# Cross-attention's output product on 13 flat tiles of 128 tokens, fed through memory

## The chip, the core and the metric

One core of a Trainium2 chip runs the whole program. The metric is the device time of one execution, in microseconds (us). TensorE is called PE below, VectorE DVE, ScalarE ACT, GpSimd POOL, and SyncE, which issues most of the DMAs, SP. A matrix product is TensorE's `lhsT.T @ rhs`: `lhsT` is loaded first (its width, up to 128 columns, is the height of the result), then `rhs` streams through, one column after the other.

## What is computed

A decoder layer on 16 batches of 100 tokens, 512 wide: self-attention, cross-attention to a context of 361 tokens per batch, and a mixture-of-experts feed-forward, each with a residual and a layer norm. The change is in the middle one, and in how its tokens are numbered for the last one:

```python
x = _layernorm(x + _L0_attn_ref(x, w_q, w_k, w_v, w_o))
# cross-attention, 16 query heads of 128 over 4 key/value heads
q = rmsnorm((x @ Wq + bq) split into 16 heads); k = rmsnorm(ctx @ Wk + bk); v = ctx @ Wv + bv
scores = einsum('bhsd,bhed->bhse', q, k) / sqrt(128)
out = einsum('bhse,bhed->bhsd', softmax(scores + mask), v)       # [16, 16, 100, 128]
x = _layernorm(x + out.reshape(16, 100, 2048) @ Wo)              # Wo: [2048, 512]
# feed-forward: logits = x @ router_w + router_b, the two best of 8 experts for each token,
# silu(x @ expert_w + expert_b), weighted sum, proj, residual, rms norm; then layernorm
```

## The kernel before, in words

Three phases follow each other: self-attention (to about 430 us of the trace), cross-attention (to about 1256 us), feed-forward. Each engine runs its own list of instructions in program order, and they meet at semaphores. Every float32 product of cross-attention is made of three matmuls (`product3`, line 67 on; the matmul is L75): each operand is split into a high and a low part in fp32r, and high times high, high times low and low times high are added in the PSUM bank.

Cross-attention is written as `body(j, par)` for batch j = 0 to 15, with a last, short `body(16, 0)`. A batch has four **steps** s = 0 to 3, one for each key/value head with its four query heads; step n = 4j + s counts them through. In step n PE does:

- for each of the four heads: `scores` into one of two banks, `transpose_probs` (L946) of one chunk of the probabilities of step n - 1, and a filler, `quarter(q)`;
- products for the keys of the next batch (`keys`, chunk 1 in the quarters of step 2, chunk 0 in step 1, chunk 2 at the end of step 2), their transposes (`transpose_keys`, L986, in steps 2 and 3), and the values of this batch (`values`, step 0);
- `values_product(n - 1)`, probabilities times values, into `o_bank`.

DVE and ACT take that bank apart into `b_oTh` and `b_oTl` (L1164 on ACT, L1299 on DVE, which adds to `o_lo`), laid out [128, 4, 400]: head width on the partitions, four heads of 100 tokens of one batch. `output(j, kv, heads)` multiplies them with `Wo`: for each batch 16 heads of three matmuls, `lhsT` 128x100, `rhs` 128x512, added up in `y_bank`. The 16 heads of a batch lie as fillers: 4 in the quarters of step 0 and 4 in those of step 1 (heads of the batch before), 1 in step 2, 7 in step 3.

The softmax of step n: `masked` on DVE (L1227, row maximum), `exponent` on ACT (L1113), `invert_sums` on DVE (L1233), `normalise` on POOL (L1402), and then PE may transpose in step n + 1. Between heads 2 and 3 DVE also does `queries(n + 1)` (L1238): it scales the queries of the next step, which SP's `load_q` (L872, L873) has loaded; ACT and POOL split them (L1119, L1391). In step 2 DVE then runs `key_squares(j + 1, 1)`, whose first instruction (L1190) empties the bank that `keys(j + 1, 2)` on PE waits for (`k_ev`).

In SP's list of before `load_q(n + 1)` waits only for the scores of step n - 1 (`s_done`). Each batch ends with `residual_norm` and `apply_norm` on DVE, the store of x2, and, two batches later, `transpose_x2` (L1006) and `logits` (L1013) on PE, all on 100 rows. The feed-forward ranks the logits, counts places for 16 batches of 100 tokens, and gathers rows of x2 by expert; the chosen places go through memory (`pick_d`) from [100, 16] to [128, 13].

Of the kernel before, what the change touches and what calls it, by code (L numbers as in the profile page):

```python
# [26 lines left out]
P = 128  # L27
# [28 lines left out]
ROUTE_WIDTHS = (S, P, NJ, E * E, NT, B)  # L56
ROUTE_COLS = sum(ROUTE_WIDTHS)
ROUTE_SPANS = [(sum(ROUTE_WIDTHS[:k]), sum(ROUTE_WIDTHS[:k + 1])) for k in range(len(ROUTE_WIDTHS))]

# [684 lines left out]
def cross_attention_phase(nc, sem, head, stage, ctxT, Wo, bv, mask, ident_s, router_w, router_b, route_c, expert_w, Ehl, x1_d, q_d, rs_d, x2_d):  # L744
# [6 lines left out]
    with ExitStack() as ctx:  # L751
# [13 lines left out]
        mask_s = sb("b_mask", [S, SE])  # L765
# [5 lines left out]
        carry = sb("b_carry", [S, XG + 1])  # L771
# [6 lines left out]
        with nc.sbuf_tensor("b_equal", [S, (B - 1) * E * E], F32) as equal_s:  # L778
            pass
        kTh = sb("b_kTh", [P, 2, XKV, SEP + 1], F32R)  # L780
        with nc.sbuf_tensor("b_above", [S, (B - 1) * E * E], F32) as above_s:
            pass
# [5 lines left out]
        oTh, oTl = sb("b_oTh", [P, XKV, XG * S], F32R), sb("b_oTl", [P, XKV, XG * S], F32R)  # L788
        x1_s, y_s = sb("b_x1", [S, D]), sb("b_y", [S, D])
        stat, mv, rstd = sb("b_stat", [S, 6]), sb("b_mv", [S, 2]), sb("b_rstd", [S, 1])  # L790
# [15 lines left out]
        y_done, ysum, stat_set, mv_set = sem("b_y_done"), sem("b_ysum"), sem("b_stat_set"), sem("b_mv_set")  # L806
# [8 lines left out]
        rb_s = stage[0:S, 0, 0, DC * E:(DC + 1) * E]  # L815
        x2T = stage[:, 0, 1, 0:DC * S]
# [25 lines left out]
        def routed(j):  # L842

            return not (isinstance(j, int) and j < 2)
# [16 lines left out]
        def _(sp):  # L861
# [20 lines left out]
            sp.dma_start(mask_s[:], mask).then_inc(consts, 16)  # L882

            def body(j, par):
                first, last, past = kinds(j)
                if not past:
                    load_q(4 * j + 1, 1, 16 * j)
                    if first:
                        load_weights(KV_PIECES)
                        load_weights(KV_PIECES + 1)  # L890
                    if not last:
                        load_ctx(j + 1, 0)
                        load_ctx(j + 1, 1)
                    load_q(4 * j + 2, 0, 16 * j + 4)
                    if first:
                        load_weights(KV_PIECES + 2)
                        load_weights(KV_PIECES + 3)
                    if not last:
                        load_ctx(j + 1, 2)
                    if last:  # L900
# [4 lines left out]
                    load_q(4 * j + 3, 1, 16 * j + 8)  # L905
                    if first:
                        load_weights(KV_PIECES + 4)
                        load_weights(KV_PIECES + 5)
                    wait(sp, ysum, j)
                    sp.dma_start(x1_s[:], x1_d[bass.ds(j, 1)].rearrange("a t d -> t (a d)")).then_inc(x1_in, 16)  # L910
                if not past and not last:
                    load_q(4 * j + 4, 0, 16 * j + 12)
                if not first:
                    sp.wait_ge(x2_rdy, j)
                    sp.dma_start(x2_d[bass.ds(j - 1, 1)].rearrange("a t d -> t (a d)"), y_s[:]).then_inc(x2_out, 16)
                if first:
                    load_weights(KV_PIECES + 6)
                    load_weights(KV_PIECES + 7)
                    sp.wait_ge(w_lo, len(pieces))
                    sp.dma_start(rw_s, router_w).then_inc(router_in, 16)  # L920
                    sp.dma_start(rb_s, router_b.partition_broadcast(S)).then_inc(router_in, 16)
                    sp.dma_start(cst, route_c).then_inc(router_in, 16)
            over_batches(sp, body)

        @block.tensor
        def _(pe):
# [63 lines left out]
            def output(j, kv, heads=range(XG)):  # L990

                if heads[0] == 0:
                    pe.wait_ge(o_lo, 4 * j + kv + 1)
                if kv == 0 and heads[0] == 0:
                    wait(pe, ysum, j)
                mm = product3(pe, y_bank[0:S, :], lambda h: oTh[:, kv, h * S:(h + 1) * S],
                              lambda h: oTl[:, kv, h * S:(h + 1) * S], lambda h: Woh[:, XG * kv + h, :],
                              lambda h: Wol[:, XG * kv + h, :], heads, first=kv == 0 and heads[0] == 0,
                              last=kv == XKV - 1 and heads[-1] == XG - 1)
                if kv == XKV - 1 and heads[-1] == XG - 1:  # L1000
                    mm.then_inc(y_done, 1)

            def transpose_x2(b):
                pe.wait_ge(x2_rdy, b + 1)
                for c in range(DC):
                    mm = pe.transpose(kv_bank[0][:, c * S:(c + 1) * S], y_s[:, c * P:(c + 1) * P], ident_s[0:S, 0:S])  # L1006
                mm.then_inc(rt_done, 1)

            def logits(b):
                pe.wait_ge(router_in, 48)  # L1010
                pe.wait_ge(rt_ev, b + 1)
                for c in range(DC):
                    mm = pe.matmul(kv_bank[0][0:S, DC * S:DC * S + E], lhsT=x2T[:, c * S:(c + 1) * S], rhs=rw_s[:, c, :],  # L1013
# [12 lines left out]
            def body(j, par):  # L1026
                first, last, past = kinds(j)
                for s in range(1 if past else 4):
                    n, before = 4 * j + s, not (first and s == 0)
                    now = not past  # L1030
                    def quarter(q):

                        if s < 2 and not first:
                            output(j - 1, s + 2, (q,))
                        if s == 2 and not last:
                            keys(j + 1, 1, (q,))
                        if s == 3:
                            output(j, (q + 1) // XG, ((q + 1) % XG,))

                    for h in range(3):  # L1040
# [9 lines left out]
                        if s == 0 and h == 0 and routed(j):  # L1050
                            transpose_x2(j - 2)
                        if s == 0 and h == 2 and routed(j):
                            logits(j - 2)
# [5 lines left out]
                    if s == 0 and now and not first:  # L1059
                        if routed(j):  # L1060
                            pe.wait_ge(lg_ev, j - 1)
                        values(j, 0)
                    if s == 1 and not last:
                        keys(j + 1, 0)
                    if s >= 2 and first:
                        pe.wait_ge(w_lo, KV_PIECES + 2 * (s - 1))
                    if s == 2:
                        output(j, 0, range(1))
# [3 lines left out]
                    if s == 3:  # L1072
                        output(j, 1, range(1, 2))
# [5 lines left out]
                    if s == 3:  # L1079
                        output(j, 1, range(2, XG))  # L1080
                if past:
                    output(j - 1, 3)
                    pe.wait_ge(lg_ev, B - 1)
                    transpose_x2(B - 1)
                    logits(B - 1)
                elif first:
                    pe.wait_ge(w_lo, len(pieces))
# [3 lines left out]
        def _(act):  # L1091
# [29 lines left out]
            def x2_transposed(b):  # L1121
                act.wait_ge(rt_done, b + 1)
                wait(act, lg_done, b)
                if isinstance(b, int) and b == 0:
# [1017 lines left out]
```

## Time and profile before

| | |
|---|---|
| time of 3 runs | 1463.97, 1468.15, 1470.35 us (median 1468.15) |
| the profiled execution: its own time, its span | 1479.52 us, 1477.7 us |
| busy share of the span: PE, DVE, ACT, POOL | 94%, 57%, 48%, 41% |
| mean granted TensorE clock | 0.976 of 2.4 GHz |
| DMA: moved, mean share of the 16 DMA engines | 126.56 MB, q1 (SP's queue) 24.3% |
| output product of cross-attention | 768 matmuls of 128x100 by 128x512 |

A busy PE isn't PE at its peak: the busy times of matmuls overlap, and what one costs is the distance from its start to the next one's. From 500 to 1200 us, 14 of the 16 batches, the profile repeats about every 50.1 us; the rows below are from one such batch.

### The profile page before, as it was taken

The numbers are of one execution on the slowest core, as the hardware profiler recorded it, in microseconds if no ns is written. First come the engines' busy times: TensorE is split into PE (matmuls) and PEld (weight loads), VectorE is DVE, ScalarE is ACT, GpSimd is POOL, SyncE is SP. The second block draws the span as 40 slices with busy tenths as digits, with TensorE's granted clock in tenths as the row PEclk, the third lists the DMA queues.
The fourth block names the chain that finished last, engine by engine and source line by source line (L and its number), as shares of the span: only waits on it lengthen the run. The fifth ranks groups of instructions, "written<-read, shape, count | busy, mean of one in ns | idle before, by whom it ended". The sixth has DMA issues, their size and how long they took to land. (4 is left out here: it accounts for less than half of the span.)

```text
span 1477.7 us, 24718 instructions
## 1 busy us (share of the span) xinstructions
PE 1390.1 (94%) x8497; PEld 1174.2 (79%) x8497; DVE 841.9 (57%) x3014; ACT 711.3 (48%) x1877; POOL 611.3 (41%) x940
## 2 busy tenths in 40 slices
PE   8999999999978999999999999999999997499976
PEld 7789888888857888888888888888888876377854
DVE  4553434344356667666755765576567655744357
ACT  5755555554434444444444444454445444343246
POOL 1632211121126455545544554545454535434154
PEclk9999999999988999999999999999999999699998
DMA  6212112122334221222121212211221130765362
GB/s 202 93 38 74 59 55 73 52 68 82 132 103 120 65 60 40 65 60 59 35 77 49 70 36 66 60 59 47 65 60 51 55 117 25 260 194 169 111 220 100
DMA packets 67475, 126.56 MB, mean 86 GB/s; under 512 B 11835, under 2 KB 42911, under 8 KB 66456
## 3 DMA queue, kind: packets, MB, share of 16 engines
q1 hardware_dynamic: 62776, 110.04, 24.3%
q0 software_dynamic: 4576, 14.95, 3.6%
q8 instruction: 69, 1.13, 0.3%
q14 instruction: 54, 0.44, 0.1%
HBM read 93.50 MB, written 31.45 MB: 85 GB/s over the span
## 5 line engine op out<-in xcount | busy, mean ns | idle before, releaser
L1113 ACT ACTIVATE b_probs<-b_probs,b_nmax 100x361 f32<-100x361 f32 x256 | 152.6, 596 | 68.7 <-DVE b_nmax L1227 67.4
L75 PE MATMUL bank<-b_kTh,b_q 128*100 128x362 f32 x512 | 172.7, 338 | 8.6 <-POOL b_q L1391 5.3
L1370 POOL TENSOR_TENSOR b_pcarry<-b_half 128x1 f32<-128x1 f32 x173 | 37.6, 217 | 343.7 <-DVE b_rinv L1233 322.0
L1227 DVE CUSTOM_DVE_ANT_0 b_probs<-bank,b_mask 100x361 f32<-100x361 f32 x256 | 135.4, 529 | 69.4 <-issue 61.4
L1108 ACT ACTIVATE b_pTh<-bank 121x400 fp32r<-121x400 f32 x192 | 95.8, 500 | 126.5 <-PE bank L946 125.6
L1402 POOL TENSOR_SCALAR b_probs<-b_probs,b_rinv 100x361 f32<-100x361 f32 x256 | 153.7, 613 | 0.0
L1220 DVE TENSOR_TENSOR b_pTl<-bank,b_pTh 121x400 fp32r<-121x400 f32 x192 | 109.7, 572 | 38.4 <-ACT b_pTh L1108 38.3
L946 PE MATMUL bank<-ident,b_probs 100*121 100x100 f32 x768 | 111.8, 268 | 7.6 <-POOL b_probs L1402 7.0
L946 PEld LDWEIGHTS bank<-ident,b_probs 100*121 100x121 f32 x768 | 106.0, 186 | 15.3 <-POOL b_probs L1402 12.5
L75 PE MATMUL bank<-b_Woh,b_oTh 128*100 128x512 f32 x256 | 110.8, 433 | 1.4 <-DVE b_oTl L1299 1.4
L440 ACT ACTIVATE a_probs<-a_probs,a_nmax 100x100 f32<-100x100 f32 x256 | 93.2, 366 | 36.7 <-DVE a_nmax L561 36.5
L1164 ACT ACTIVATE b_oTh<-bank,b_bv 128x400 fp32r<-128x400 f32 x64 | 38.1, 596 | 139.9 <-PE bank L75 139.9
L75 PEld LDWEIGHTS bank<-b_kTh,b_q 128*100 128x100 f32 x512 | 85.3, 167 | 22.9 <-POOL b_q L1391 6.8
L75 PE MATMUL bank<-b_Wol,b_oTh 128*100 128x512 f32 x256 | 100.8, 394 | 0.0
L75 PE MATMUL bank<-b_Woh,b_oTl 128*100 128x512 f32 x256 | 100.6, 393 | 0.0
L606 DVE TENSOR_SCALAR a_qb<-bank,a_bq,a_qkw 128x400 f32<-128x400 f32 x64 | 44.3, 693 | 94.6 <-PE bank L75 94.6
L75 PE MATMUL bank<-a_x1Th,a_Wqh 128*128 128x400 f32 x256 | 91.7, 358 | 0.2 <-ACT a_qsq L464 0.2
L75 PE MATMUL bank<-a_x1Tl,a_Wqh 128*128 128x400 f32 x256 | 88.3, 345 | 0.0
L75 PE MATMUL bank<-a_x1Th,a_Wql 128*128 128x400 f32 x256 | 88.3, 345 | 0.0
L706 POOL TENSOR_TENSOR a_probs<-a_probs,a_rinv 100x400 f32<-100x400 f32 x64 | 54.6, 855 | 73.0 <-DVE a_rinv L568 73.0
L75 PE MATMUL bank<-b_Wkh,b_ctxh 128*121 128x512 f32 x192 | 81.2, 423 | 3.5 <-DVE b_kn L1190 3.5
L75 PE MATMUL bank<-b_kTl,b_q 128*100 128x362 f32 x256 | 84.4, 330 | 0.0
(256 smaller groups left out, 3793.9 us busy)
## 6 DMA issues: line engine op xcount, KB each, us to landing
q_d<-a_qb SPq DMA_DIRECT2D x64, 200.0 KB, 2.4
b_q_raw<-q_d SPq DMA_DIRECT2D x64, 200.0 KB, 2.5
b_q_raw<-rs_d SPq DMA_DIRECT2D x64, 200.0 KB, 3.4
b_ctxr<-in_ctxT SPq DMA_DIRECT2D x48, 242.0 KB, 4.5
y_d<-c_y SPq DMA_DIRECT2D x32, 256.0 KB
c_Eraw<-in_expert_w SPq DMA_DIRECT2D x10, 512.0 KB, 7.4
a_stage<-in_Wq SPq DMA_DIRECT2D x4, 1024.0 KB
stage<-in_Wo SPq DMA_DIRECT2D x8, 512.0 KB, 4.5
```

The costliest lines, as they stand in the source:

```text
L75: mm = eng.matmul(out, lhsT=l(c), rhs=r(c), start=first and k == 0, stop=last and k == n - 1)
L440: e = act.activation(probs[:, r, c, :], probs[:, r, c, :], ACT.Exp, scale=-1.0, bias=nmax[:, h:h + 1], accum_out=psums[:, r, c:c + 1])
L606: dve.tensor_scalar(qb[:, u % 2, :, m % XG, :], q_bank(m)[:, 0:GT].rearrange("p (b t) -> p b t", b=GB), bq_s[:, m % XH:m % XH + 1], qkw_s[ ...
L706: pool.tensor_tensor(probs[:, r], probs[:, r], rinv[:, r].unsqueeze(2).to_broadcast([S, DC, S]), ALU.mult).then_inc(pn_rdy, 1)
L946: mm = pe.transpose(t_bank[c % 2][0:KT, h * S:(h + 1) * S], probs[:, s % 2, h, c * KT:(c + 1) * KT], ident_s[0:S, 0:S])
L1108: act.activation(pTh[:, c, :], t_bank[c % 2][0:KT, 0:XG * S], ACT.Copy).then_inc(pt_hi, 1)
L1113: act.activation(p, p, ACT.Exp, scale=-1.0, bias=nmax[:, s % 2, h:h + 1], accum_out=psums[:, s % 2, h:h + 1]).then_inc(e_rdy, 1)
L1164: act.activation(oTh[:, kv, :], o_bank[:, 0:XG * S], ACT.Identity, bias=bv_s[:, kv:kv + 1]).then_inc(o_hi, 1)
L1220: dve.tensor_tensor(pTl[:, c, :], t_bank[c % 2][0:KT, 0:XG * S], pTh[:, c, :].bitcast(F32), ALU.subtract).then_inc(pt_lo, 1)
L1227: dve.tensor_tensor_reduce(out=probs[:, s % 2, h, 0:SE], in0=s_bank[h % 2][0:S, 0:SE], in1=mask_s[:], scale=-1.0, scalar=BIG, op0=ALU.add, ...
L1370: pool.tensor_tensor(pcarry[:, k:k + 1], half_s[:, 0:1], half_s[:, 0:1], ALU.add)
L1402: pool.tensor_scalar(p, p, rinv[:, s % 2, h:h + 1], 1.0, ALU.mult, ALU.mult).then_inc(p_rdy, 1)
```

## The change

The output product no longer works batch by batch. The 1600 tokens are cut into 13 tiles that ignore batches: tile 0 has 64 rows (`SHORT`), the others 128. Since a tile takes rows of two or three batches, what `values_product` gives is stored in DRAM (`o_d`, `store_values`, after `o_lo`) and loaded back by tiles (`load_group` into `b_oD0`, `b_oD1`). A **group** is a tile and a key/value head: 4 heads, 12 matmuls with `lhsT` 128x128. `output_plan` gives each group a step, at most one in a step (two in step 63), none in a step 2 before step 36. Of the last tile only 28 columns come from memory; 100 are written in place. The residual, the norms, the transposes, the logits and the routing work on the 13 tiles with 128 partitions, and `pick_d` is gone.

```diff
+def output_plan():
+    order = [(t, kv) for t in range(NT) for kv in range(XKV)]
+    plan, g = {}, 0
+    while order:
+        plan[g] = []
+        room = 2 if g == 4 * B - 1 else 0 if g % 4 == 2 and g < 36 else 1
+        while order and room:
+            t, kv = order[0]
+            ready = 4 * last_batch(t) + kv + (2 if t == NT - 1 else 3)
+            if ready > g:
+                break
+            plan[g].append(order.pop(0))
+            room -= 1
+        g += 1
...
+            def load_group(t, kv):
+                k = slot(t, kv)
...
+                    wait(sp, y_grp, taken(t, kv))
+                if t < NT - 1:
+                    sp.wait_ge(o_out, 16 * (4 * last_batch(t) + kv + 1))
+                    src = o_d[kv][:, :, :, tile_start(t):tile_start(t) + tile_rows(t)]
+                    sp.dma_start(oD[k][:, :, :, 0:tile_rows(t)].bitcast(F32), src).then_inc(od_in[k], 16)
...
+            def store_values(n):
+                sp.wait_ge(o_lo, n + 1)
+                sp.dma_start(o_d[n % 4][:, :, :, n // 4 * S:(n // 4 + 1) * S], oT[:].bitcast(F32)).then_inc(o_out, 16)
...
+                for s in range(1 if past else 4):
+                    g = 4 * j + s
+                    if g + 1 < 4 * B:
+                        load_q(g + 1, (g + 1) % 2, 4 * g)
...
+                    for t, kv in PLAN.get(g + 1, ()):
+                        load_group(t, kv)
...
+                    if 1 <= g <= 4 * (B - 1):
+                        store_values(g - 1)
...
-                        if s < 2 and not first:
-                            output(j - 1, s + 2, (q,))
                         if s == 2 and not last:
                             keys(j + 1, 1, (q,))
-                        if s == 3:
-                            output(j, (q + 1) // XG, ((q + 1) % XG,))
+                        for t, kv in groups:
+                            if len(groups) > 1:
+                                if q % 2 == 0:
+                                    output(t, kv, (q, q + 1))
+                            elif s < 3 or q < 2:
+                                output(t, kv, (q,))
...
                     if s == 2:
-                        output(j, 0, range(1))
                         values_product(n - 1, s - 1, j)
...
-                    if s == 3:
-                        output(j, 1, range(1, 2))
                     if before and s != 2:
                         values_product(n - 1, (s + 3) % 4, j)
...
-                    if s == 3:
-                        output(j, 1, range(2, XG))
+                    if s == 3 and len(groups) == 1:
+                        for t, kv in groups:
+                            output(t, kv, range(2, XG))
...
-                    if s == 1 and not first:
-                        residual_norm(j - 1)
...
+                    if n in DONE[:-1]:
+                        residual_norm(DONE.index(n))
```

By the plan the groups lie: one in every step 0 from step 4 on but for 48, one in every step 1 from step 5 on but for 13 and 49, one in every step 3 (two in 63), and one in the steps 2 numbered 38, 42, 46, 54, 58 and 62; two more in steps 64 and 65. `DONE`, the steps in which a tile's last group lies, is 7, 12, 19, 24, 29, 35, 39, 43, 47, 54, 58, 62, 65.

PE, the end of a step 3, from the last matmul of the scores over `transpose_keys(2)` (reads `b_kn`) to the product with the values. Before:

```order
L75 MATMUL bank<-b_kTh,b_q 100x362
L986 MATMUL bank<-ident,b_kn 128x121 x4
L75 MATMUL bank<-b_Woh,b_oTh 100x512
L75 MATMUL bank<-b_Wol,b_oTh 100x512
L75 MATMUL bank<-b_Woh,b_oTl 100x512
L75 MATMUL bank<-b_Woh,b_oTh 100x512
L75 MATMUL bank<-b_Wol,b_oTh 100x512
L75 MATMUL bank<-b_Woh,b_oTl 100x512
L75 MATMUL bank<-b_pTh,b_Vh 128x400
```

The same place after:

```order
L122 MATMUL bank<-b_kTh,b_q 100x362
L1075 MATMUL bank<-ident,b_kn 128x121 x4
L122 MATMUL bank<-b_pTh,b_Vh 128x400
L122 MATMUL bank<-b_pTl,b_Vh 128x400
L122 MATMUL bank<-b_pTh,b_Vl 128x400
```

Two heads (six matmuls) between the key transposes and the product with the values are gone; a third is gone between scores 2 and 3.

SP, one batch of a middle part, from a step 1 to the next step 0. Before:

```order
L872 DMA b_q_raw<-q_d 128x400
L873 DMA b_q_raw<-rs_d 128x400
L868 DMA b_ctxr<-in_ctxT 128x484
L872 DMA b_q_raw<-q_d 128x400
L873 DMA b_q_raw<-rs_d 128x400
L910 DMA b_x<-x_d 100x512
```

After:

```order
L973 DMA o_d<-b_oT 1024x1x100
L935 DMA b_q_raw<-q_d 128x400
L936 DMA b_q_raw<-rs_d 128x400
L931 DMA b_ctxr<-in_ctxT 128x484
L973 DMA o_d<-b_oT 1024x1x100
L935 DMA b_q_raw<-q_d 128x400
L936 DMA b_q_raw<-rs_d 128x400
L956 DMA b_oD<-o_d 128x8x128
```

Each pair of query loads now stands behind a store of the heads' values, 1024 pieces of 100 elements (400 KB), and so behind that store's wait for `o_lo`.

## Rows read from the trace of the kernel before

**Rows 1.** The page, engines: busy time, share of the span, number of instructions

```profile
PE 1390.1 (94%) x8497; PEld 1174.2 (79%) x8497; DVE 841.9 (57%) x3014; ACT 711.3 (48%) x1877; POOL 611.3 (41%) x940
```

**Rows 2.** One batch's steps 0 to 3: stretch, length, busy (count), clock, DMA, GB/s

```profile
839.20:856.70 17.50, 17.25 (x95) 14.32 (x94) 6.75 (x23) 6.36 (x16) 8.30 (x15) 1.00 0.37 102
856.70:867.10 10.40, 10.40 (x59) 8.98 (x58) 7.61 (x29) 4.99 (x13) 3.55 (x7) 1.00 0.25 57
867.10:878.70 11.60, 11.60 (x66) 10.12 (x65) 8.91 (x36) 6.29 (x15) 8.17 (x14) 1.00 0.14 40
878.70:889.30 10.60, 10.60 (x64) 8.91 (x63) 9.27 (x34) 6.04 (x15) 5.20 (x11) 1.00 0.00 0
```

**Rows 3.** Who waited for whom, whole span: us in total, times, longest

```profile
PE bank L946 <- POOL b_probs L1402: 7.0, 17, 2.5
```

**Rows 4.** PE in order of time, step 2 and its end: start, length, instruction

```profile
873.55 0.39 PE L75 MATMUL bank<-b_Woh,b_oTh 128*100 128x512 f32 x1
...
874.23 0.34 PE L75 MATMUL bank<-b_pTh,b_Vh 121*128 121x400 f32 x1
...
875.86 0.40 PE L75 MATMUL bank<-b_Wkh,b_ctxh 128*121 128x512 f32 x1
...
878.64 0.33 PE L75 MATMUL bank<-b_kTh,b_q 128*100 128x362 f32 x1
```

**Rows 5.** PE in order of time, the start of the next step 0

```profile
890.18 0.67 PE L946 MATMUL bank<-ident,b_probs 100*121 100x100 f32 x4 [0.25 <-POOL b_probs L1402]
...
891.38 0.51 PE L1006 MATMUL bank<-ident,b_y 100*128 100x100 f32 x4
...
894.91 0.79 PE L1013 MATMUL bank<-stage 128*100 128x8 f32 x8
```

**Rows 6.** DVE in order of time, end of step 1 and step 2

```profile
867.91 0.63 DVE L1299 SCALAR_TENSOR_TENSOR b_oTl<-bank,b_bv,b_oTh 128x400 fp32r<-128x400 f32 x1 [0.35 <-ACT b_oTh L1164]
...
872.45 0.57 DVE L1238 TENSOR_TENSOR b_q_raw<-b_q_raw 128x400 f32<-128x400 f32 x1
...
874.32 0.67 DVE L1190 TENSOR_TENSOR b_kn<-bank,bk 121x512 f32<-121x512 f32 x1
```

**Rows 7.** DVE in order of time, end of step 2 and step 3

```profile
878.91 0.69 DVE L1190 TENSOR_TENSOR b_kn<-bank,bk 121x512 f32<-121x512 f32 x1 [1.34 <-PE bank L75]
...
880.61 0.53 DVE L1227 CUSTOM_DVE_ANT_0 b_probs<-bank,b_mask 100x361 f32<-100x361 f32 x1
...
886.16 0.16 DVE L1233 RECIPROCAL b_rinv<-b_psums 100x2 f32<-100x2 f32 x1
```

**Rows 8.** POOL in order of time, the last of step 3

```profile
888.83 1.29 POOL L1402 TENSOR_SCALAR b_probs<-b_probs,b_rinv 100x361 f32<-100x361 f32 x2
```

**Rows 9.** SP in order of time: a query load, and the store of picks

```profile
862.15 0.32 SPq L872 DMA_DIRECT2D b_q_raw<-q_d x1
...
1283.11 0.57 SPq L1600 DMA_DIRECT2D pick_d<-c_pick_b x1
```

**Rows 10.** DMA issues of 862 to 868 us: count, KB, us to landing

```profile
b_q_raw<-rs_d SPq DMA_DIRECT2D x1, 200.0 KB, 3.4
```

**Rows 11.** DMA issues of 838.8 to 845 us, the same columns

```profile
x_d<-b_y SPq DMA_DIRECT2D x1, 200.0 KB
...
b_q_raw<-rs_d SPq DMA_DIRECT2D x1, 200.0 KB, 4.3
```

**Rows 12.** SP's queue from 1311 to 1313 us: packets, MB, share of 16 engines

```profile
q1 hardware_dynamic: 1725, 0.24, 72.9%
```

**Rows 13.** Busy time and clock in batch 0, as in rows 2

```profile
456.00:460.00 4.00, 1.53 (x9) 0.92 (x7) 3.86 (x6) 1.28 (x2) 3.76 (x4) 1.00 0.32 79
...
468.00:472.00 4.00, 0.54 (x3) 0.24 (x3) 3.74 (x4) 1.97 (x4) 4.00 (x4) 1.00 0.26 55
472.00:476.00 4.00, 4.00 (x12) 3.01 (x11) 1.38 (x9) 0.00 (x0) 1.27 (x3) 0.57 0.57 213
```

**Rows 14.** DVE in the routing, and the ranking ahead of it

```profile
1252.16 1.15 DVE L1334 TENSOR_TENSOR b_equal<-b_equal,stage 100x960 f32<-100x960 f32 x1
...
1267.41 4.62 DVE L1842 TENSOR_TENSOR c_Q<-c_p,c_iota 100x1024 bf16<-100x1024 bf16 x4
```

More of the change, by code:

```diff
@@ L840, in kinds, with slot, loads, taken @@
             return [isinstance(j, int) and j == k for k in (0, B - 1, B)]
-        def routed(j):
-            return not (isinstance(j, int) and j < 2)
+        def slot(t, kv):
+            return 2 + kv if t == NT - 1 and kv < 2 else kv % 2
+        def loads(t, kv):
+            return 16 if slot(t, kv) > 1 else 16 * (2 * t + kv // 2 + (0 if t == NT - 1 else 1))
+        def taken(t, kv):
+            return 4 * t + kv - (3 if t == NT - 1 else 1)
+        def attended(n):
+            return [(oT[:, k] if n < 4 * (B - 1) else oD[slot(NT - 1, n % 4)][:, k, :, LEFT:P]) for k in range(2)]
         def key_bank(jn, c):
@@ L892, in body @@
                         load_ctx(j + 1, 0)
                         load_ctx(j + 1, 1)
[L894 to L898, printed above, removed]
+                    if s == 1 and not last:
                         load_ctx(j + 1, 2)
-                    if last:
+                    if s == 1 and last:
                         sp.wait_ge(v_done, KC * B)
@@ L988, in transpose_keys, with output @@
                 mm.then_inc(kt_done, 1)
-            def output(j, kv, heads=range(XG)):
+            def output(t, kv, heads):
+                n, k = tile_rows(t), slot(t, kv)
                 if heads[0] == 0:
[L993 to L1001, printed above, removed]
@@ L1003, in transpose_x2 @@
-            def transpose_x2(b):
-                pe.wait_ge(x2_rdy, b + 1)
+                    pe.wait_ge(od_in[k], loads(t, kv))
+                    if t == 0:
+                        pe.wait_ge(w_lo, KV_PIECES + 2 * (kv + 1))
+                    if t == NT - 1:
+                        pe.wait_ge(o_lo, 4 * (B - 1) + kv + 1)
+                    if kv == 0:
+                        wait(pe, ysum, t)
+                mm = product3(pe, y_bank[0:n, :], lambda h: oD[k][:, 0, h, 0:n], lambda h: oD[k][:, 1, h, 0:n],
+                              lambda h: Woh[:, XG * kv + h, :], lambda h: Wol[:, XG * kv + h, :], heads,
+                              first=kv == 0 and heads[0] == 0, last=kv == XKV - 1 and heads[-1] == XG - 1)
@@ L1572, in feed_forward_phase @@
         NP = len(pieces)
-        def rows(t):
-            return P if t < NT - 1 else B * S - P * (NT - 1)
+        rows = tile_rows
         def weight_of(t, k):
@@ L2096, in layouts @@
         np.broadcast_to(np.where(np.arange(NT) > 0, np.arange(NT) * P, -1), (P, NT)),
-        token,
+        np.broadcast_to([tile_start(t) // (P - SHORT) for t in range(NT)], (P, NT)),
+        np.arange(P)[:, None],
     ], 1).astype(np.float32)
```

389 lines of the change are left out of this document (222 added, 167 removed).

## The prediction

> **What bounds the kernel now.** I read the page first: PE is busy 94% of the span [rows 1], but that alone says nothing about what 144 fewer matmuls are worth. So I read one batch of the repeating part step by step. In all four steps PE is busy for practically the whole stretch, at the full clock of 2.4 GHz, while DVE is busy 6.75 to 9.27 us of 10 to 17 [rows 2]. Then I asked which wait ends last. PE has one wait that returns in every batch: the first transpose of probabilities in step 0 waits 0.25 us for POOL's `normalise` [rows 5]; over the span such waits are 17, 7.0 us in all [rows 3]. It is short, but it says that at the end of step 3 a chain of other engines is exactly as long as PE's work. The chain starts when PE ends the third chunk of keys, at 878.64 [rows 4], which I call E. DVE has idled 1.34 us for it, starts at 878.91, and from there its instructions stand one behind the other (key squares, four `masked`, two key norms, three splits, the queries) to the reciprocal at 886.16 [rows 7]; POOL's last `normalise` runs from 888.83 to 890.12 [rows 8], and PE transposes at 890.18 [rows 5]. So **from E to the transposes of the next step 0 is 11.54 us, whatever PE does in step 3**, and the rest of the 50.1 us, 38.6 us, from there through steps 0, 1 and 2 to the next E, is PE's own work.
>
> **What a head costs.** Three matmuls of the output product take 874.23 - 873.55 = 0.68 us from start to start [rows 4]; I use 0.69 for those between transposes too. `rhs` is 512 columns before and after, and what streams sets the distance, so I take the same for `lhsT` of 128 columns. Before there are 256 heads, after 13 x 16 = 208: 48 fewer, 33 us of PE's work. Where they go decides.
>
> **Step 3: 44 of the 48 heads, worth nothing.** A batch had 7 heads in step 3 and has 4 (8 in step 63). Fifteen batches lose 3 heads, 2.1 us each. All of it lies between E and the transposes, where PE has 0.25 us of slack in the wrong direction: it now waits about 2.3 us instead. None of DVE's or POOL's instructions in the chain is removed (`apply_norm` stood behind it). Sum: 0.
>
> **Step 2, light (batches 1 to 8 and 12): one head less, -0.7, and a new stall.** `load_q` now stands behind `store_values`, which waits for `o_lo`. Of the four steps three don't mind: there DVE needs the queries 6 us or more after that store. In step 2 it does. DVE ends `b_oTl` of step 1 at 867.91 + 0.63 = 868.54 and wants the queries at 872.45 [rows 6]; before, they were issued at 862.15 [rows 9], now 6.8 us later. The store's issue costs 0.3 to 0.57 us (the store of picks, with 1600 pieces, took 0.57 [rows 9]); I take 0.4, so the first load goes out at 869.0 and the second 0.36 later. The second lands 3.4 us after its issue with nothing ahead [rows 10] and 4.3 us with a store of 200 KB ahead [rows 11], 0.9 us for 200 KB. The new store has 400 KB: 869.36 + 3.4 + 1.8 = 874.6. It also comes in 1024 pieces, 64 for each of 16 DMA engines; a small packet cost 0.729 x 2 us x 16 / 1725 = 13.5 ns [rows 12], 0.86 us for 64, so 875.4 if none of that overlaps. I take 875.0: DVE stands still for 2.55 us. The lower bound is 872.8 (no transfer ahead counts), 0.3 us. Behind it on DVE are `masked` of head 3, the reciprocals and L1190, which ended at 874.32 + 0.67 = 874.99 [rows 6] and now at 877.54. PE's third chunk of keys needs that bank; it began at 875.86 [rows 4], would begin at 875.2 with a head less, and begins at 877.6. So E comes 1.7 us later than before. Nine such batches: **+15.3**; with the lower bound, where PE doesn't wait, 9 x -0.7 = -6.3.
>
> **Step 2, full (batches 9, 10, 11, 13, 14): three heads more.** Here 4 heads stand where 1 stood, on the part that is PE's own: 5 x 2.1 = **+10.5**. The stall hides: with a head between the scores DVE asks for the queries 1.4 us later, and with the keys' third chunk 2.1 us later the bank is free in time. In steps 54 and 58 `residual_norm` (1.65 us on DVE) stands between `b_oTl` and the key squares, 1.0 us more than the 1.34 us that DVE idled there [rows 7] and the shift allow: **+2**.
>
> **Steps without a group.** Steps 13, 48 and 49 lose four heads each on PE's own part: 12 x 0.69 = 8.3; I take **-8**, as DVE must follow.
>
> **Tiles instead of batches.** The transposes of x2 cost 0.28 us and the logits 0.65 (distances behind the rows at 891.38 and 894.91 [rows 5]); three fewer of each: **-2.8**. In the routing, DVE's chain shrinks by 3/16 where it counts batches: `c_Q` 4.62 us [rows 14] becomes 3.75, the four operations on Zone and cmp give 0.7, the ranking three of 1.15 us [rows 14] give 0.7; two short memsets are added: **-2**. `pick_d` was not waited for, so its removal gives nothing.
>
> **Ends.** In the last batch step 62 gets three heads among scores that are bound by POOL, and step 63 one: **+1.5**. Other costs I put at nothing: group loads are issued a step ahead with 10 us of cover; a store has 6 us before ACT writes `b_oT` again; `residual_norm` behind a step 3 delays `masked` of step 0, which has over 6 us before anything waits.
>
> **Sum**: 15.3 + 10.5 + 2 - 8 - 2.8 - 2 + 1.5 = +16.5. The span becomes 1494.2 us and that execution 1496.0; it ran 11.4 us above the median of the runs, so the median is 1468.15 + 16.5 = 1484.7, **1485 us**.
>
> **Rivals.**
> 1. *PE's work is what is saved.* If the chain from E were not fixed (DVE's row of instructions gets shorter when PE is less in its way), all 48 heads count, -33, with the tiles -38: **1430**. For it speaks only that PE is busy throughout [rows 2]; against it the wait that is there in each batch [rows 3, 5]. It decides if step 3 shrinks from 10.6 to about 8.5 us. 8%.
> 2. *The queries come in time.* Then the light batches give 0.7 us each: 16.5 - 15.3 - 6.3 = -5.1, **1463**. For it: only 0.3 us are certain. Against: 400 KB ahead in the same queue. 17%.
> 3. *The small pieces are slow.* If a 400-byte write costs the engines twice as long, the store takes 2.1 us more; the stall is 4.65 us, E is 3.8 us late in nine batches (+18.9 more) and 2 us in the five full ones (+10): **1514**. No row shows such a write, the nearest is rows 12. 10%. The Trainium skill ("DMA: Bandwidth & Descriptors", Specifications) gives 512 bytes as the least transfer for line rate, with a read-modify-write below it; by it this rival would be the forecast.
> 4. *The clock falls.* PE will stand still for about 2.4 us in step 2. In batch 0 a stretch with 0.54 us of work in 4 was followed by one at 0.57 of full speed, that is mostly at 1.2 GHz, in which 12 key matmuls took about 4.4 us and not 2.8; a stretch with 1.53 us of work in 4 was not followed by a fall [rows 13]. If each of nine stalls costs 1.6 us: +14, **1499**. 15%. The Trainium skill ("TensorE: Matmul & The Clock Gate", Why this matters for your kernels) advises against long idle gaps between bursts; by the gap of 2.4 us it leaves my sum as it is.
>
> **Chances and range.** The forecast has 50%. About 0.5% (7.3 us) is what a measurement of this kernel can tell from no change. Faster than 1460.8: rival 1 and a quarter of rival 2, 12%. Within: the rest of rival 2 and the low edge of my forecast, 19%. Slower than 1475.5: 69%. The range from 1461 to 1508 leaves out rival 1 and its neighbours below (12%) and rival 3 above (8%); its inside takes in a stall from 0.3 us to 4 us.
>
> **What would show it.** In the trace of the changed kernel: step 3 stays near 10.5 us and PE waits there, in pieces, for about 2.3 us (else rival 1); DVE idles before the queries' product in step 2 for a DMA, 1.5 to 3.5 us, in the batches with a light step 2 and not in steps 0 and 1 (none: rival 2; over 4 us: rival 3); the third chunk of keys waits for DVE's copy of the second; batches 9 to 11 take about 52 us at the full clock (half clock in step 2: rival 4); and the distance between output matmuls stays at 0.23 us. I would be wrong altogether if DMA traffic, which rises by some 50 MB, slowed the context loads or the group loads so that PE waits for them in steps that I hold for unchanged.

## The result, and the profile after

| kernel | median us | runs | against before (interval) |
|---|---|---|---|
| before | 1468.99 | 4 | |
| changed | 1510.03 (1509.24 to 1511.95) | 4 | 1.0278 (1.0262 to 1.0294) |

The change costs 41.0 us. I had forecast 16.5 us, so the direction held and the size didn't; 1510 lies outside the range.

The page of the changed kernel, engines, with DMA packets and SP's queue; the first row answers to [rows 1]:

```profile
PE 1388.1 (92%) x8311; PEld 1169.7 (78%) x8311; DVE 840.6 (56%) x3000; ACT 709.7 (47%) x1875; POOL 604.8 (40%) x934
...
DMA packets 180860, 175.67 MB, mean 116 GB/s; under 512 B 80164, under 2 KB 156296, under 8 KB 179841
...
q1 hardware_dynamic: 176160, 159.16, 38.6%
```

PE has 186 instructions fewer and is busy for only 2 us less: a matmul at half clock is busy for longer, and with the queries in time (e1, below) the same instructions are busy for 1374.8 us. The other engines did what they did before; what grew is the time in between.

**Step 2 of a batch without a group in that step (batch 5).** DVE and PE in order of time, with SP's three issues ahead of them; the columns are start, length, instruction and the idle time before it:

```profile
732.26 0.53 SPq L973 DMA_DIRECT2D o_d<-b_oT  x1
733.14 0.35 SPq L935 DMA_DIRECT2D b_q_raw<-q_d  x1
733.54 0.87 SPq L936 DMA_DIRECT2D b_q_raw<-rs_d  x1
```
```profile
731.60 0.63 DVE L1403 SCALAR_TENSOR_TENSOR b_oT<-bank,b_bv,b_oT 128x400 fp32r<-128x400 f32 x1 [0.50 <-ACT b_oT L1269]
...
738.83 0.58 DVE L1343 TENSOR_TENSOR b_q_raw<-b_q_raw 128x400 f32<-128x400 f32 x1 [2.63 <-DMA b_q_raw<-rs_d]
...
740.70 0.67 DVE L1295 TENSOR_TENSOR b_kn<-bank,bk 121x512 f32<-121x512 f32 x1
```
```profile
741.52 0.47 PE L122 MATMUL bank<-b_Wkh,b_ctxh 128*121 128x512 f32 x1 [2.51 <-DVE b_kn L1295]
...
742.38 0.63 PE L122 MATMUL bank<-b_Wkh,b_ctxh 128*121 128x512 f32 x1
...
745.92 0.32 PE L122 MATMUL bank<-b_kTh,b_q 128*100 128x362 f32 x1
```

This is the chain of the prediction, link by link: the store is issued as soon as DVE's part of `b_oT` (`b_oTl` before) is there (731.60 + 0.63 = 732.23, and 732.26), the queries behind it, DVE stands 2.63 us for them (2.55 forecast), its copy of the second chunk comes late, and PE waits 2.51 us for the bank ([rows 4, 6] show both without a wait). But then the twelve key matmuls, which took 2.78 us in [rows 4], take 745.92 - 741.52 = 4.40 us. The stretches around it, two microseconds each, with the columns of [rows 2] (the granted clock stands behind POOL's busy time):

```profile
738.00:740.00 2.00, 1.01 (x6) 0.68 (x4) 1.11 (x5) 0.56 (x2) 0.00 (x0) 1.00 0.78 230
740.00:742.00 2.00, 0.48 (x2) 0.46 (x3) 1.23 (x3) 1.54 (x4) 1.98 (x4) 1.00 0.00 0
742.00:744.00 2.00, 2.00 (x6) 1.51 (x6) 1.92 (x9) 0.00 (x0) 1.97 (x5) 0.54 0.00 0
744.00:746.00 2.00, 2.00 (x7) 1.48 (x6) 0.00 (x0) 0.00 (x0) 1.02 (x1) 0.61 0.43 116
```

PE worked 1.49 us of 4, and behind that the clock is at 0.54 and 0.61, that is mostly at 1.2 GHz: rival 4, on top of the forecast. Such a fall follows in five of the nine batches with this stall (1, 2, 3, 5 and 6: 14.9 to 15.7 us for the step). In the other four (4, 7, 8 and 12) the step takes 12.8 to 13.4 us at full clock. In batch 4, one of them, the same place reads 1.01 and 0.89 busy and no fall behind it:

```profile
686.00:688.00 2.00, 1.01 (x6) 0.67 (x4) 1.11 (x5) 0.97 (x3) 0.39 (x2) 1.00 0.81 237
688.00:690.00 2.00, 0.89 (x4) 0.78 (x5) 1.65 (x5) 1.13 (x4) 2.00 (x4) 1.00 0.00 0
690.00:692.00 2.00, 2.00 (x11) 1.54 (x10) 1.52 (x9) 0.00 (x0) 1.92 (x5) 1.00 0.00 0
```

**Where the 41 us come from.** I cut both traces at the first score matmul of each of the 64 steps, and took the kernel before from a second trace (e4, below), whose span agrees with the median. Step 63 starts 41.1 us later in the changed kernel; the rest of the program takes the same to 0.2 us. In us, against before:

| part | changed | queries first (e1) | forecast |
|---|---|---|---|
| step 2, no group (9) | +25.0 | -3.3 | +15.3 |
| step 2, with a group (5) | +11.0 | +10.7 | +10.5, +2 |
| step 3 (14) | -5.6 | -6.7 | 0 |
| steps 0 and 1 of batches 2 to 14, and step 5 | +0.3 | +0.2 | -8, -2.8 |
| start to step 4 | +3.7 | +1.3 | 0 |
| steps 60 to 62 | +6.7 | +6.0 | +1.5 |
| step 63 and behind it | -0.2 | -0.7 | -2 |

### The profile page after: what moved, and what is told of

It is laid out like the page before. It is cut to its first block and busy times, and to the rows that moved or that the text cites. A ratio compares the mean times of both kernels' runs of the same rounds, so it can differ in the third digit from the quotient of the medians.

```text
span 1508.2 us, 24533 instructions
## 1 busy us (share of the span) xinstructions
PE 1388.1 (92%) x8311; PEld 1169.7 (78%) x8311; DVE 840.6 (56%) x3000; ACT 709.7 (47%) x1875; POOL 604.8 (40%) x934
## 2 busy tenths in 40 slices
DMA packets 180860, 175.67 MB, mean 116 GB/s; under 512 B 80164, under 2 KB 156296, under 8 KB 179841
## 3 DMA queue, kind: packets, MB, share of 16 engines
q8 instruction: 68, 1.11, 0.3%
## 5 line engine op out<-in xcount | busy, mean ns | idle before, releaser
L122 PE MATMUL bank<-b_kTh,b_q 128*100 128x362 f32 x512 | 175.8, 344 | 8.8 <-POOL b_q L1502 5.6
L122 PE MATMUL bank<-b_Woh,b_oD 128*128 128x512 f32 (+1 forms) x400 | 167.4, 426 | 3.9 <-DMA b_oD<-o_d 2.5
L1035 PE MATMUL bank<-ident,b_probs 100*121 100x100 f32 x768 | 113.7, 271 | 16.5 <-POOL b_probs L1522 16.0
L122 PE MATMUL bank<-b_Wkh,b_ctxh 128*121 128x512 f32 x192 | 85.5, 445 | 25.3 <-DVE b_kn L1295 25.3
L122 PEld LDWEIGHTS bank<-b_Woh,b_oD 128*128 128x128 f32 (+1 forms) x400 | 75.2, 188 | 16.5 <-DMA b_oD<-o_d 2.6
L1502 POOL TENSOR_TENSOR b_q<-b_q_raw,b_q 128x400 fp32r<-128x400 f32 x64 | 68.6, 1072 | 33.0 <-ACT b_q L1218 33.0
L122 PE MATMUL bank<-b_Wol,b_oD 128*128 128x512 f32 (+1 forms) x200 | 80.0, 400 | 0.0
```

What stands on the lines that cost most here:

```text
L122: mm = eng.matmul(out, lhsT=l(c), rhs=r(c), start=first and k == 0, stop=last and k == n - 1)
L1035: mm = pe.transpose(t_bank[c % 2][0:KT, h * S:(h + 1) * S], probs[:, s % 2, h, c * KT:(c + 1) * KT], ident_s[0:S, 0:S])
L1502: pool.tensor_tensor(q_s[:, n % 2, 1], q_raw[:, n % 2, 1], q_s[:, n % 2, 0].bitcast(F32), ALU.subtract).then_inc(q_lo, 1)
```

## The experiments

All stand beside runs of the kernel before on the same chip (medians of 1468.0 to 1469.7 us).

**e1: the queries ahead of the store.**

```diff
                     if g + 1 < 4 * B:
                         load_q(g + 1, (g + 1) % 2, 4 * g)
+                    if 2 <= g <= 4 * (B - 1) + 1:
+                        store_values(g - 2)
...
-                    if 1 <= g <= 4 * (B - 1):
-                        store_values(g - 1)
```

> The store of a step's values is issued behind the queries of the step after next instead of ahead of them; nothing else changes. Theory A (the order on SP's queue makes the stall): DVE no longer waits for a DMA in the nine light steps 2, they fall from 13.3-15.6 us to about 10.8 us (before: 11.5 us, and a head less), 9 x (2.8 + 0.7) = about -31 us against the changed kernel: 1479 us. Theory B (the traffic itself, 400-byte pieces, slows the queries wherever they stand): step 2 stays above 13 us and the time at 1505-1512 us.

Measured: 1476.12 us (1475.39 to 1476.73), 33.9 us less than the changed kernel, 1.0053 (1.0034 to 1.0072) of the kernel before. DVE and SP in the same step 2 of batch 5, and below them the step as one stretch, of the changed kernel and of this one:

```profile
715.19 0.54 SPq L973 DMA_DIRECT2D o_d<-b_oT  x1
...
719.04 0.57 DVE L1343 TENSOR_TENSOR b_q_raw<-b_q_raw 128x400 f32<-128x400 f32 x1
```
```profile
730.77:745.92 15.15, 12.64 (x62) 10.62 (x61) 8.82 (x34) 6.17 (x15) 8.15 (x14) 0.89 0.44 103
```
```profile
713.70:724.57 10.87, 10.87 (x62) 9.52 (x61) 8.74 (x34) 6.29 (x15) 7.47 (x14) 1.00 0.49 124
```

The wait of DVE is gone, PE is busy for the whole step, and seven of the nine steps take 10.9 to 11.0 us, one head less than before (11.54). The other two, 12.0 us in batch 3 and 12.2 in batch 7, have no wait for queries either; PE waits there 0.76 us for POOL and 0.53 us for `b_kn`. The same bytes move in the same pieces, so it was the order in SP's queue. The order is worth more than the nine stalls (25.0 + 3.3 = 28.3 us): step 2 of batch 0, where DVE waited 1.68 us for queries too, gives another 1.9 us, step 4 1.3, and steps 55 and 59 together 1.0.

**e2: the stall filled.**

```diff
                         values_product(n - 1, s - 1, j)
+                        if not groups and not first and not last:
+                            keep_busy(pe, t_bank[1][:, 0:P], ident_s, 10)
```

> Ten matmuls of 128 columns on a free bank (about 2.1 us of TensorE work) stand between the values' product and the third chunk of keys in steps 2 that have no group; the stall itself stays. Theory A (the granted clock falls because PE stands still there): the five steps that took 15.0-15.6 us fall to 13.3 us, about -10 us: 1500 us. Theory B (the clock falls for another reason, or the longer steps come from the bank and not from the clock): no gain, 1510 us, or up to 9 x 0.5 us more where the filling is longer than the stall.

Measured: 1505.97 us (1505.44 to 1506.3), 4.1 us less than the changed kernel. PE in step 2 of batch 5, and the clock around it:

```profile
736.41 2.39 PE L130 MATMUL bank<-ident 128*128 128x128 f32 x20
738.88 0.47 PE L122 MATMUL bank<-b_Wkh,b_ctxh 128*121 128x512 f32 x1
...
741.73 0.32 PE L122 MATMUL bank<-b_kTh,b_q 128*100 128x362 f32 x1
```
```profile
738.00:740.00 2.00, 1.93 (x13) 1.57 (x12) 1.86 (x7) 0.90 (x2) 2.00 (x5) 1.00 0.00 0
740.00:742.00 2.00, 2.00 (x11) 1.58 (x10) 1.29 (x7) 0.00 (x0) 1.92 (x4) 1.00 0.00 0
```

The clock stays at 1.00, and the twelve key matmuls take 741.73 - 738.88 = 2.85 us again, 1.55 us less than at the half clock (rival 4 had 1.6). All nine steps now take 13.4 to 14.2 us, at a clock of 1.00 in each: no fall is left. So the fall comes from PE standing still. The gain is smaller than I expected (4 for 10 us). The five steps with a fall give 7.4 us, and the four that had kept their clock lose 0.1 to 0.9 us each, 1.9 together: in batch 7 the filling (2.47 us here) is longer than the wait that it fills (1.11), and in batches 4 and 8 DVE's wait for the queries was itself 0.4 and 0.6 us longer than in the changed kernel. The clock's own part in the changed kernel is what its five steps take above 13.3 us, the mean of batches 4, 8 and 12, which have the stall alone: 9.5 us, of which 1.1 belongs to the other wait in step 14 (e1 has it too), so about 8.4 us. The Trainium skill ("TensorE: Matmul & The Clock Gate", Why this matters for your kernels) advises against long idle gaps between bursts. The prediction read it as leaving this gap out of account; here a wait of 2.51 us was followed by the half clock, and so was one of 1.90 us, and the measurement decides.

**e5: the store in whole pieces.** `o_d` is laid out by batch, so that the store writes 3200 bytes in one piece for each partition, and a group load picks its tile out of two or three batches:

```diff
-    o_d = nc.dram_tensor("o_d", (XKV, P, 2, XG, B * S), F32, kind="Internal").ap()
+    o_d = nc.dram_tensor("o_d", (XKV, P, B, 2, XG, S), F32, kind="Internal").ap()
...
-                sp.dma_start(o_d[n % 4][:, :, :, n // 4 * S:(n // 4 + 1) * S], oT[:].bitcast(F32)).then_inc(o_out, 16)
+                sp.dma_start(o_d[n % 4][:, n // 4], oT[:].bitcast(F32)).then_inc(o_out, 16)
...
-                    src = o_d[kv][:, :, :, tile_start(t):tile_start(t) + tile_rows(t)]
-                    sp.dma_start(oD[k][:, :, :, 0:tile_rows(t)].bitcast(F32), src).then_inc(od_in[k], 16)
+                    for b, b0, t0, n in parts(t):
+                        sp.dma_start(oD[k][:, :, :, t0:t0 + n].bitcast(F32), o_d[kv][:, b, :, :, b0:b0 + n]).then_inc(od_in[k], 16)
```

> The changed kernel with o_d laid out by batch: the store writes 128 pieces of 3200 bytes instead of 1024 of 400, and the group loads pick their tiles out of two or three batches, in short pieces. Theory A (the stall comes from the order and from 400 KB ahead of the queries; pieces count 0.9 us at most): the store lands after about 3.7-4.5 us, the wait in light steps 2 shrinks by 0 to 0.9 us, the time falls by 0 to 10 us, 1500-1510 us. Theory B (rival 3: the small pieces make the stall): the store lands after less than 3.3 us and the light steps 2 fall below 12.5 us, 25 us or more, 1485 us or less.

Measured: 1492.31 us (1490.49 to 1493.61), 17.7 us less than the changed kernel, between the two. DMA issues of the changed kernel and of this one, the median time to landing last, and DVE's wait for the queries in this one's batch 5:

```profile
o_d<-b_oT SPq DMA_DIRECT2D x60, 400.0 KB, 4.6
...
b_q_raw<-rs_d SPq DMA_DIRECT2D x64, 200.0 KB, 5.2
```
```profile
o_d<-b_oT SPq DMA_DIRECT2D x60, 400.0 KB, 2.7
...
b_q_raw<-rs_d SPq DMA_DIRECT2D x64, 200.0 KB, 4.5
```
```profile
727.61 0.57 DVE L1356 TENSOR_TENSOR b_q_raw<-b_q_raw 128x400 f32<-128x400 f32 x1 [1.34 <-DMA b_q_raw<-rs_d]
```

The same 400 KB land in 2.7 and not 4.6 us: the pieces of 400 bytes cost the store 1.9 us. The queries behind it gain less, 1.3 us in batch 5: the second load is issued 0.87 and not 1.31 us behind DVE's part of `b_oT`, because SP is through with the store's issue after 0.33 us (0.53) and with the first load's 0.4 us sooner, and it lands 4.4 and not 5.3 us after its issue. For the pieces I had allowed at most 0.86 us and taken half. For the 400 KB themselves I had 1.8 us, and they cost about 1.0 (4.4 us against the 3.4 of [rows 10]). I also had the second load issued 0.82 us behind `b_oTl`. These errors cancel, and the stall came out as forecast, 2.63 for 2.55 us. Rival 3 was right that short pieces are dearer than I took them for, but its stall of 4.65 us didn't come. That its 1514 us lies near the measured 1510 is chance. PE's wait is now 0.6 to 1.25 us, and all nine steps 2 without a group run at a clock of 1.00: they take 11.9 to 12.8 us, 7.3 us together above the kernel before, where the changed kernel had 25.0. So a stall that is half as long costs less than half. The Trainium skill ("DMA: Bandwidth & Descriptors", Specifications) gives 512 bytes as the least transfer for line rate; the two landing times agree with it for a write. The short pieces of the group loads, which are now shorter still (122019 packets under 512 bytes, and 80164 in the changed kernel), have cover and no step shows them.

**e6: the store alone, in the kernel before.** Each step's values are also written to a tensor that nobody reads, at the changed kernel's place in SP's order:

```diff
+            def store_values(n):
+                if 0 <= n < 4 * (B - 1):
+                    sp.wait_ge(o_lo, n + 1)
+                    dst = o_d[n % 4][:, :, :, n // 4 * S:(n // 4 + 1) * S]
+                    sp.dma_start(dst, oT[:, n % 4].rearrange("p k (h t) -> p k h t", h=XG).bitcast(F32)).then_inc(o_out, 16)
...
+                    store_values(4 * j)
                     load_q(4 * j + 3, 1, 16 * j + 8)
```

> The kernel before, which also writes each step's values to memory, in the changed kernel's pieces and at the changed kernel's place in SP's order; nobody reads them, all else is as before. Theory A (that place is the whole stall): steps 0, 1 and 3 stay, step 2 of 14 batches takes 1.7 us more, and 3.5 us more where the clock falls (in 5 of 9 before): 14 x 1.7 = 24 us to 14 x 3.5 = 49 us, 1493-1518 us. Theory B (the stall belongs to the group loads and tiles): within 5 us of the kernel before.

Measured: 1512.9 us (1510.99 to 1516.79), 1.030 (1.0271 to 1.0329) of the kernel before: +43 us. PE in step 2 of batch 5:

```profile
741.89 0.47 PE L75 MATMUL bank<-b_Wkh,b_ctxh 128*121 128x512 f32 x1 [2.18 <-DVE b_kn L1203]
```

Steps 1 and 3 stay as they were, step 0 but for one that took 1.2 us more, and step 2 of all fourteen batches takes 13.3 to 15.5 us for 11.54, 38.7 us together; six of them are over 15 us. The stall needs neither the group loads nor the tiles, only the store's wait and its bytes ahead of the queries. Added alone, this part of the change costs +43 us, where the whole change costs +41; but here fourteen steps have the stall, and in the changed kernel nine.

**e3: two groups in step 3.** On top of e1, steps 28, 29, 38, 42 and 46 lose their group to step 3 of batches 5, 6, 9, 10 and 11 (a further condition, not shown, keeps a pair within one tile, and the two groups' heads are spread over the quarters):

```diff
-        room = 2 if g == 4 * B - 1 else 0 if g % 4 == 2 and g < 36 else 1
+        room = 2 if g == 4 * B - 1 or g % 4 == 3 and 12 < g < 60 else 0 if g % 4 == 2 and g < 54 else 1
```

> On top of queries first: two groups (8 heads) in step 3 of batches 5, 6, 9, 10 and 11, so that steps 28, 29, 38, 42 and 46 have none. Theory A (heads in step 3 are covered by the chain from the keys' third chunk up to 7 heads, heads elsewhere cost 0.69 us each): 20 heads less on PE's own part, -13.8 us, plus about 5 x 0.4 us for the eighth head: -12 us against queries first, about 1467 us. Theory B (a head costs the same everywhere): 0 against queries first.

Measured: 1471.54 us (1467.43 to 1473.85), 4.6 us less than e1, where 12 was expected. Step 3 of batch 5 and the step 0 behind it in this kernel, and step 3 of the same batch in the changed kernel:

```profile
724.06:735.39 11.33, 11.33 (x67) 10.12 (x65) 8.83 (x32) 5.71 (x14) 4.46 (x9) 1.00 0.49 121
735.39:752.81 17.42, 16.54 (x83) 13.62 (x81) 9.15 (x27) 6.67 (x16) 9.44 (x17) 1.00 0.59 160
```
```profile
745.92:756.07 10.15, 9.35 (x54) 7.72 (x53) 8.76 (x33) 5.92 (x15) 3.60 (x7) 1.00 0.46 114
```

With 4 heads step 3 takes 10.15 us and PE idles 0.80 of it; with 7 it took 10.63 (e4; 10.60 in the rounded cuts of [rows 2]); with 8 it takes 11.33 and is full. So the first three heads are worth 0.48 us and the eighth its 0.70: the second group costs 1.18 us, where I had 0.4. I had set the chain at a fixed length, but it became a little longer too: where the tile ends in step 3, `residual_norm` stands in front of the next step 0, which takes 17.42 and not 16.87 us. The ones that lost their group paid as priced (38: 13.68 to 10.89; 28: 18.18 to 15.03). In this trace step 48 takes back another 2.4 us (14.11 to 16.53): PE has no group there and now waits 0.93 us for DVE, and the clock falls behind that wait (0.90 over the step); in e7, with the same plan, the step takes 15.01 us at full clock. Neither theory: a head in step 3 is cheap up to seven, not free.

**e4: the kernel before once more.**

> The kernel before, once more, for a second trace. If the profiled execution of before was disturbed behind 1256 us, this one reaches the same place at the same time and ends about 9 us earlier (span about 1466 us); if it is the kernel, its feed-forward part takes the same 9 us more than that of the changed kernel again.

Measured: 1469.11 us, span 1467.3 us; the first trace had 1477.7. The two agree to 1.5 us up to step 63. Behind it, from 1380 to 1420 us, the first trace and this one read:

```profile
1380.00:1420.00 40.00, 30.00 (x181) 25.71 (x180) 10.74 (x16) 8.64 (x16) 13.64 (x14) 0.93 0.49 161
```
```profile
1380.00:1420.00 40.00, 37.94 (x224) 31.29 (x223) 18.83 (x36) 13.77 (x28) 19.79 (x21) 1.00 0.59 193
```

Of the 10 us by which the first one ran over its median 8.9 lay behind the start of step 63, in the feed-forward part; the change has no share in them, and the table above is made with this trace.

**e7: the end and step 4.** On top of e3. `load_group` for step 62 is moved ahead of the six loads of expert weights, and ten matmuls fill the wait at the start of step 4:

```diff
                     if s == 1 and last:
+                        for t, kv in PLAN.get(g + 1, ()):
+                            load_group(t, kv)
                         sp.wait_ge(v_done, KC * B)
...
+                        if n == 4 and h == 0:
+                            keep_busy(pe, t_bank[1][:, 0:P], ident_s, 10)
```

> On top of e3: the group of step 62 is loaded ahead of the 3 MB of expert weights, and ten matmuls of 128 columns fill PE's wait at the start of step 4. Theory A (step 62's 5.3 us more are the wait for that load and the half clock behind it; step 4's are the wait of 2.5 us and the half clock behind it): step 62 falls from 14.5 to about 11 us (9.2 plus three heads less what POOL bounds), step 4 from 18.7-20.3 to 17.5-18.5 us, about -5 us: 1466 us. Theory B (DMA traffic at the end sets the time, the load only moves the wait): 1471 us.

Measured: 1467.76 us (1464.97 to 1469.64), 0.9981 (0.9968 to 0.9995) of the kernel before. PE's waits in step 62 of the changed kernel, the clock behind them, and the first wait of step 63 here; then step 62 as one stretch, here and in e8, the next experiment, where it holds the same four heads:

```profile
1255.27 0.79 PE L122 MATMUL bank<-b_Woh,b_oD 128*128 128x512 f32 x1 [2.45 <-DMA b_oD<-o_d]
...
1265.95 0.41 PE L122 MATMUL bank<-b_kTh,b_q 128*100 128x362 f32 x1 [1.04 <-POOL b_q L1502]
```
```profile
1253.00:1255.00 2.00, 0.00 (x0) 0.00 (x0) 0.57 (x1) 0.93 (x3) 0.00 (x0) 0.79 1.12 366
1255.00:1257.00 2.00, 1.73 (x4) 1.40 (x5) 0.00 (x0) 0.00 (x0) 0.00 (x0) 0.50 1.04 186
1257.00:1259.00 2.00, 2.00 (x9) 1.87 (x8) 0.54 (x3) 0.37 (x1) 0.00 (x0) 0.50 0.41 55
```
```profile
1223.83 0.41 PE L122 MATMUL bank<-b_kTh,b_q 128*100 128x362 f32 x1 [1.04 <-POOL b_q L1509]
```
```profile
1212.51:1223.82 11.31, 9.77 (x45) 8.23 (x45) 5.17 (x20) 5.39 (x14) 3.51 (x8) 0.85 0.57 161
```
```profile
1207.14:1216.86 9.72, 8.19 (x45) 6.92 (x45) 5.16 (x20) 5.38 (x14) 3.51 (x8) 1.00 0.66 184
```

In the changed kernel the group stands behind 3 MB; PE waits 2.45 us for it and then works at the half clock: 15.04 us for the step. With the load ahead PE waits for no DMA there, and the step takes 11.31 us, 2.1 us above before (9.21). That looks like three heads at full price, but it isn't: the clock is at 0.85 over the step here, and in e8 the same step at full clock takes 9.72. So the three heads cost 0.5 us between POOL's waits at both ends of the step, and the half clock 1.6. Why it falls here and not in e8, no run settles. In step 4 the wait is down to 0.27 us and the step takes 18.75 us, as it did in e3 without the filling; e1 had 20.32 and the changed kernel 21.62. So there the filling gave nothing over e3, whose clock had held by itself; what e7 gives is the load, 3.2 us in the traces (14.55 to 11.31).

**e8: a table by hand.** On top of e7, pairs in step 3 of eleven batches (steps 51, 55 and 59 keep their one group), and fourteen filling matmuls in step 2 of batch 0:

```diff
+STARTS = ((4, 5, 7, 7), (11, 11, 15, 15), (16, 17, 19, 19), (20, 21, 23, 23), (27, 27, 31, 31), (32, 33, 35, 35),
+          (36, 37, 39, 39), (40, 41, 43, 43), (44, 45, 47, 47), (51, 52, 53, 54), (55, 56, 57, 58), (59, 60, 61, 62), (63, 63, 64, 65))
...
+    for t, steps in enumerate(STARTS):
+        for kv, g in enumerate(steps):
+            plan[g].append((t, kv))
```

> On top of e7: a table by hand puts two groups in step 3 of eleven batches (five in e7) and none in step 3 of the others, 23 groups in steps 0, 1 and 2 and not 28; fourteen matmuls of 128 columns fill PE's wait in step 2 of batch 0. By the prices that e3 showed (a group elsewhere 2.76 us, the second group in step 3 1.15 us, a tile that ends in step 3 another 0.6 us in step 0): -5 x 2.76 + 6 x 1.15 + 4 x 0.6 - 2 = -6.5 us, and up to -2 us for the clock in step 2: 1459-1462 us. Rival (the chain from the keys' third chunk becomes longer by other work where step 3 is full, or early pairs fall on the weights' split): 1466-1470 us.

Measured: 1461.35 us (1460.53 to 1462.16), 0.9953 (0.9939 to 0.9967) of the kernel before: inside the 1459 to 1462 us worked out from e3's prices. It is the fastest kernel of this study, 6.6 us ahead of the 1468.0 us of the kernel before beside it. Step 2 of batch 0 fell from 21.41 to 19.04 us, and step 12, which has no group left, from 17.86 to 13.94. That the sum fits so closely is partly luck. Between the two traces the moved groups give 3.4 us, where the prices had 4.5, and the start gives 1.9; another 1.6 come from step 62, which this edit doesn't touch and whose clock held this time.

## Why the prediction was wrong, point by point

**What bounds the kernel: right.** Step 3 went from 10.63 to 10.15 us when it lost three of seven heads, and from E to the transposes it is 11.36 us and no longer 11.54, in twelve of fourteen batches. PE idles there, in pieces (in batch 5 0.35 us for `b_kn`, 0.32 us for `b_pTl`, 0.50 us for POOL in front of the transposes). That is 1.3 us with what is idle in smaller pieces, and not the 2.3 that I gave as a sign; part of the difference is only in the counting, since a matmul's row lasts 0.39 us where the next starts 0.23 behind it, and a wait shows that much shorter. Rival 1 (8.5 us for the step) falls. The term of 0 measured -5.6 us in the changed kernel's steps 3, of which 3.3 us come back as a longer wait for POOL in step 0 (0.50 for 0.25 us, thirteen times).

**Step 2 without a group: right mechanism, +25.0 us for +15.3.** The stall itself was forecast well: in batches 4, 8 and 12, which kept their clock, the step is 1.7 to 1.9 us longer than before, for a forecast of 1.7. That was partly luck, since its prices were wrong in opposite directions (e5). The step of the prediction that failed here is the choice to make the clock a rival with 15%, and to leave it out of the sum: it cost 8.4 us (e2). In the prediction [rows 13] showed a fall behind a stretch with 0.54 us of work in 4 and none behind 1.53 us. The stall that I forecast leaves 1.6 us of work in 4, beside the row without a fall, and I took that one row for more than it could carry: in batch 5 a fall came behind 1.49 us in 4, and in batch 4 none behind 1.90. Seen from now, an even chance for each of nine stalls at 1.6 us would have put 7 us into the sum; that is an estimate.

**Step 2 with a group: right**, +11.0 for +10.5. The +2 for `residual_norm` in steps 54 and 58 measured 1.0: it shows as 0.46 and 0.56 us more in steps 55 and 59, and e1 hasn't got it.

**Empty steps and tiles: +0.3 us for -10.8.** Steps 13, 48 and 49 gave 6.7 us (8 forecast). The rest is +7.0 where I had -2.8: the step that failed is the price of a tile, which I took over unchanged from batches. The tile's transposes and its logits, PE in step 21 of the changed kernel:

```profile
720.60 0.60 PE L1100 MATMUL bank<-ident,b_y 128*128 128x128 f32 x4
720.95 0.41 PE L122 MATMUL bank<-b_kTh,b_q 128*100 128x362 f32 x1
...
723.49 0.48 PE L122 MATMUL bank<-b_Woh,b_oD 128*128 128x512 f32 x1
723.81 0.39 PE L122 MATMUL bank<-b_Wol,b_oD 128*128 128x512 f32 x1
...
724.27 0.95 PE L1108 MATMUL bank<-stage 128*128 128x8 f32 x8
725.08 0.39 PE L122 MATMUL bank<-b_kTh,b_q 128*100 128x362 f32 x1
```

The transposes take 0.35 us to the next instruction and the logits 0.81, where [rows 5] had 0.28 and 0.65; a step 1 with a group and both takes 11.82 us and one without them 10.51, 1.31 more. Ten such in steps 8 to 59 make 13.1 us; thirteen of 100 tokens made 12.1 at 0.93 us each, or 13.9 us with 0.07 us for the instruction behind each of the two. I had taken three fewer at the old price: the tiles save operations, and each became dearer by nearly as much. Likewise the first output matmul behind a set of transposes now takes 0.32 us and not 0.29, three times a step, about 2 us in all: "the same for `lhsT` of 128 columns" holds in a row of matmuls and not for the first. Add POOL's 3.3 us, and 2 us in steps 12 and 24, where `residual_norm` stands ahead of `values_lo` and PE waits 0.69 us for `b_Vl`.

**Start and end: +10.4 us for +1.5.** I had put group loads at nothing, "issued a step ahead with 10 us of cover"; that step failed too. In step 62 the load stood behind 3 MB of expert weights in the same queue, and PE waited 2.45 us for it (e7). In batch 0 the queries come late as well. And where PE had waited 1.20 us at the end of step 3 for DVE's split of the output weights, it now comes earlier, by three heads, and waits 2.51 us in step 4 for POOL's `normalise`, with the half clock behind it (0.50 from 490 to 494 us). I had looked at the repeating batches alone.

**The routing: -0.2 us for -2** from step 63 on, with step 63's head more in it; no experiment here takes it apart.

In sum, the miss is 24.5 us. Above the forecast lie steps 0 and 1 (11.1), the two ends (8.9), the clock in step 2 (8.4), the routing (1.8) and the rest of step 2 without a group (1.3); below it steps 3 (5.6) and step 2 with a group (1.5).

## What to carry to other kernels

Read the order of a DMA queue as you read an engine's: before a store that waits for a result is put into it, ask what stands behind it and when that is wanted; here one swapped pair of issues was worth 34 us. When the sum gives TensorE a stall of about 2 us that it didn't have, put a fall of its clock into the sum, weighted by its chance: here it followed eleven of twenty-three waits of 1.1 to 2.85 us (five of nine, and six of fourteen in e6) and none of nine of 0.6 to 1.25 us (e5). And an edit that replaces many small operations by fewer large ones has to be priced with the large one's duration, at the first and the last batch too.

## What was new of the hardware

- 400 KB to memory landed after 4.6 us in pieces of 400 bytes and after 2.7 us in pieces of 3200 bytes (e5).
- Of PE's waits of 1.1 to 2.85 us in step 2 of the changed kernel five of nine were followed by the half clock, of those of 1.5 to 2.2 us in e6 six of fourteen, and of those of 0.6 to 1.25 us in e5 none of nine. Twelve key matmuls took 4.40 us behind such a fall and 2.85 us without. Why the longer of two waits can be the one without a fall (2.10 us without, 1.90 with one), no run here settles.
- Four transposes with 128 rows of tokens took 0.35 us to the next instruction, and four with 100 rows 0.28; the logits behind them took 0.81 and 0.65.
